# Four step sums in flight and a gather ring of 14 chunks in a four-layer graph network

## What is computed

```
h = relu(layernorm(x))
# layer 0: two graph convolutions (self-loops, 1/sqrt(deg) on both sides)
h = segment_sum((h @ W)[src] * dinv[src] * dinv[dst], dst) + b     # twice
# layer 1: 8 capsules of 16 features, three rounds of routing
z = xc[src];  u = xc
for _ in range(3):
    p = softmax(einsum('ecd,ecd->ec', z, u[dst]));  u = l2norm(segment_sum(z * p, dst) + xc)
# layer 2: mean of the neighbours
h = relu(where(deg > 0, segment_sum(h[src], dst) / deg, h) @ W + b)
# layer 3: messages with three edge attributes
m = gelu(concat(h[src], attr) @ W1 + b1) @ W2 + b2
h = layernorm(h + segment_sum(m, dst)) * gamma + beta
```

## Time and profile before

| | us |
|---|---|
| runs (3) | 6747.69, 6748.66, 6758.79; median 6748.66 |
| profiled execution, from the first to the last instruction | 7795.8 |
| busy in it: PE / DVE / ACT / POOL | 4038 / 3242 / 1099 / 4491 |

### The profile page before, as it was taken

How to read it: one execution, slowest core, us unless ns; L and a number is a source line. 1 busy time by engine, 2 the same in 40 slices (tenths; PEclk the granted TensorE clock), 3 DMA queues, 4 the chain that set the end, 5 groups by cost and what they waited for, 6 DMA issues and landing times.

```text
span 7795.8 us, 105357 instructions
## 1 busy us (share of the span) xinstructions
PE 4038.3 (52%) x24944; PEld 3239.4 (42%) x24945; DVE 3241.9 (42%) x8240; ACT 1099.4 (14%) x2520; POOL 4491.4 (58%) x4619
## 2 busy tenths in 40 slices
PE   0333334333333455555558868823333347777776
PEld 0323323333233345544557767713333334444443
DVE  4222213222124555555578888842221243333335
ACT  0000000000001222222233343310000021111112
POOL 4666665666664555555535535546666635555553
PEclk9656656556566676667789989955665565555555
DMA  3111112111111333333347757711111111111111
GB/s 98 44 45 45 45 46 54 44 46 45 45 45 29 118 118 119 118 118 119 120 151 224 225 176 228 223 47 44 45 45 45 45 41 38 38 39 38 39 38 39
DMA packets 354854, 637.41 MB, mean 82 GB/s; under 512 B 85485, under 2 KB 120442, under 8 KB 354170
## 3 DMA queue, kind: packets, MB, share of 16 engines
q0 software_dynamic: 127936, 263.97, 13.5%
q10 hardware_dynamic: 105408, 191.94, 7.9%
q1 hardware_dynamic: 121466, 181.04, 6.8%
HBM read 500.81 MB, written 135.79 MB: 82 GB/s over the span
## 4 chain that ended last, share of the span: by engine, by line
another core or an unknown queue 35%; PE 24%; issue 16%; DVE 12%; DVEq 5%; DMA 4%; ACT 3%; ACTq 1%; SPq 0%; POOL 0%; POOLq 0%
PE ps_sum L606 15%; PE ps_u L661 4%; PE ps_u L639 4%; DMA hots<-hot_rows 3%; DVE zu L1190 2%; DVE onehot L1000 2%; DVEq L241 2%; DVE acc L1014 1%; DVEq L1014 1%; DVE logit L1199 1%; ACT hots L808 1%; PE ps_a L656 1%; DVE prob_n L1174 1%; ACT onehot L818 1%
## 5 line engine op out<-in xcount | busy, mean ns | idle before, releaser
L525 POOL DMA_INDIRECT ring<-table,rows_idx x3920 | 3874.4, 988 | 2436.8 <-issue 1126.9
L606 PE MATMUL ps_sum<-ring,onehot 128*128 x5856 | 1202.3, 380 | 2328.5 <-DVE onehot L1000 1047.7
L606 PEld LDWEIGHTS ps_sum<-ring,onehot 128*128 128x128 f32 x5856 | 1078.6, 280 | 2452.1 <-issue 2450.5
L1014 DVE TENSOR_TENSOR acc<-ps_sum,acc 128x128 f32 x1708 | 492.2, 288 | 3140.0 <-remote 2336.3
L606 PE MATMUL ps_sum<-msg,onehot 128*128 128x128 f32 x7808 | 1479.8, 349 | 33.3 <-POOL msg L311 21.9
L606 PEld LDWEIGHTS ps_sum<-msg,onehot 128*128 128x128 f32 x7808 | 1285.1, 249 | 432.0 <-issue 396.5
L639 PE MATMUL ps_u<-u_parts,hots 128*128 x8784 | 763.8, 239 | 790.1 <-ACT hots L808 364.8
L1000 DVE SCALAR_TENSOR_TENSOR onehot<-dst,minus_row,iota 128x512 f32<-128x512 f32 x1220 | 913.8, 749 | 239.8 <-issue 211.9
L639 PEld LDWEIGHTS ps_u<-u_parts,hots 128*128 128x128 bf16 x8784 | 619.9, 106 | 915.0 <-issue 880.4
L311 POOL TENSOR_TENSOR msg<-ring,prob_n 128x512 f32<-128x512 f32 x488 | 516.9, 1059 | 614.6 <-DVE prob_n L1174 581.8
L1190 DVE TENSOR_TENSOR zu<-ps_u,ring 128x512 f32<-128x512 f32 x732 | 503.1, 687 | 594.8 <-remote 283.8
(11 more groups left out here) (149 smaller groups left out, 1919.9 us busy)
## 6 DMA issues: line engine op xcount, KB each, us to landing
hots<-hot_rows ACTq DMA_DIRECT2D x488, 256.0 KB, 3.5
ring<-z_rows SPq DMA_DIRECT2D x392, 256.0 KB, 3.6
ring<-table,rows_idx POOLq DMA_INDIRECT x3920
hot_rows<-hots ACTq DMA_DIRECT2D x244, 256.0 KB
z_rows<-ring SPq DMA_DIRECT2D x196, 256.0 KB
table<-acc SPq DMA_DIRECT2D x9, 1024.0 KB, 5.1
x<-in_x SPq DMA_DIRECT2D x1, 3328.0 KB, 11.6
table<-h SPq DMA_DIRECT2D x4, 832.0 KB, 4.4
```

Of the source, the lines that this page charges most:

```text
L525: nc.gpsimd.indirect_dma_start(out=ring[:, j, t * P:(t + 1) * P], out_offset=None, in_=tables[p], in_offset=bass.IndirectOffsetOnAxis(ap=r ...
L606: last = nc.tensor.matmul(ps_sum[k % 2][:, 0:P], lhsT=onehot[:, k % HOTS, t, :], rhs=rows(t), start=(t == 0), stop=(t == TILES - 1))
L1014: V.tensor_tensor(acc_flat[:, at], ps_sum[k % 2][:, 0:P], acc_flat[:, at], ALU.add)\
```

## The change

- In CONV1, CONV2, MEAN and EDGE the ring has 14 slots (`FAR`), and it lies in `u_parts` (`far_flat`) instead of `ring`. CAPS1 keeps the 7 slots of `ring`.
- In these passes SP returns chunk j - 7 behind the publication of chunk j (`far_round`), and POOL waits for the slot of the chunk 14 before.
- The plain passes (not EDGE) sum in four PSUM tiles, `plain_sums`; PE waits for the add of the step four before, and DVE adds three steps behind the onehot.
- `tmp` can't be used ahead of EDGE any more, so deg * BO is added by 52 operations, one per block.
- `rows_idx` holds 14 chunks; `key_row` and `chunk_tab` become 16 bits wide.

```diff
+FAR = 2 * RING
+SLOTS = {CONV1: FAR, CONV2: FAR, CAPS1: RING, CAPS2: RING, CAPS3: RING, MEAN: FAR, EDGE: FAR}
+        far_flat = u_parts[:, :, :, :].rearrange("p b k f -> p (b k f)").bitcast(fp32)[:, 0:FAR * TILES * P]
-        rows_idx = sb("rows_idx", [P, 2, RING, TILES], i32)
+        rows_idx = sb("rows_idx", [P, 2, FAR, TILES], i32)
-        key_row = sb("key_row", [1, CHUNKS], i32)
+        key_row = sb("key_row", [1, CHUNKS], u16)
-        chunk_tab = sb("chunk_tab", [1, 256], i32)
+        chunk_tab = sb("chunk_tab", [1, 256], u16)
+        plain_sums = (ps_sum[0], ps_sum[1], ps_u[0], ps_u[1])
...
+                def far_round(q, first):
+
+                    c0 = q * FAR
+                    for half in range(2):
+                        frees = not first or half
+                        if frees:
+                            keys = keys_of(c0 + (half - 1) * RING, RING)
+                        for j in range(RING):
+                            publish(half * RING + j, q)
+                            if frees:
+                                free(keys[j], None, None)
...
-                    for j in range(RING):
+                    for j in range(slots):
                         if not first:
-                            pool.wait_ge(slot_free, r * RING + (before_this + j + 1 - RING))
+                            pool.wait_ge(slot_free, r * slots + (before_this + j + 1 - slots))
...
-            def sum_step(s, k, p, rows):
+            def sum_step(s, k, p, rows, sums=ps_sum):
                 pe.wait_ge(hot_ready, s + (1 + STEPS * p))
-                if not (s.fixed and s + STEPS * p < 2):
-                    pe.wait_ge(step_added, s + (STEPS * p - 1))
+                if not (s.fixed and s + STEPS * p < len(sums)):
+                    pe.wait_ge(step_added, s + (STEPS * p + 1 - len(sums)))
...
             def plain_pass(p):
+                ahead = len(plain_sums) - 1
+
                 def body(s, k, chunk, have):
                     if have(0):
                         hot(s, k, chunk(0), p)
-                    if have(1):
-                        add_step(s.back(1), k - 1, chunk(1), p)
-                over_steps(dve, ENGINE.DVE, body, 1)
+                    if have(ahead):
+                        add_step(s.back(ahead), k - ahead, chunk(ahead), p, plain_sums)
+                over_steps(dve, ENGINE.DVE, body, ahead)
...
-            link(V.tensor_tensor(tmp, per_feature(BO, NB), per_row(deg[:, :], [P, NB, P]), ALU.mult))
-            link(V.tensor_tensor(h[:, :, :], h[:, :, :], tmp, ALU.add))
+            for b in range(NB):
+                last = V.scalar_tensor_tensor(out=h[:, b, :], in0=BO[:, :], scalar=deg[:, b:b + 1],
+                                              in1=h[:, b, :], op0=ALU.mult, op1=ALU.add)
+            link(last)
```

More of the change, by code:

```diff
@@ L42, with uses_before @@
 GATHERS = (CONV1, CONV2, CAPS1, MEAN, EDGE)
+SLOTS = {CONV1: FAR, CONV2: FAR, CAPS1: RING, CAPS2: RING, CAPS3: RING, MEAN: FAR, EDGE: FAR}
+def uses_before(p, j, kind):
+    return sum(CHUNKS // SLOTS[g] for g in kind if g < p and j < SLOTS[g])
 def build(nc, x_in, src_in, dst_in, dst_rows_in, row_last_in, last_row_in, last_col_in, attr_in, w1, b1, w2, b2, w_mean, b_mean,
           w_edge, b_edge, w_out, b_out, gamma, beta, out):
-    fp32, bf16, i32 = mybir.dt.float32, mybir.dt.bfloat16, mybir.dt.int32
+    fp32, bf16, i32, u16 = mybir.dt.float32, mybir.dt.bfloat16, mybir.dt.int32, mybir.dt.uint16
     ALU = mybir.AluOpType
@@ L182, in build @@
         free_seen = sem("free_seen")
-        rows_in = [sem(f"rows_in{j}") for j in range(RING)]
+        rows_in = [sem(f"rows_in{j}") for j in range(FAR)]
         rows_loaded = [sem(f"rows_loaded{j}") for j in range(RING)]
@@ L246, in block_of, with ring_at, ring_of, slot @@
             return ((s + 0) - chunk).with_bounds(min_val=0, max_val=BLOCKS - 1)
-        def ring_at(chunk):
-            return (chunk % RING) * (TILES * P)
+        def ring_at(chunk, p=CAPS1):
+            return (chunk % SLOTS[p]) * (TILES * P)
+        def ring_of(p):
+            return far_flat if SLOTS[p] == FAR else ring_flat
+        def slot(p, j):
+            return ring_of(p)[:, j * TILES * P:(j + 1) * TILES * P]
         class Step:
@@ L453, in _ @@
                     for j in range(RING - LAG, RING):
-                        publish(j, ROUNDS - 1)
-                for j in range(0 if loads else RING - LAG, RING):
-                    free(keys[j], j, ROUNDS - 1)
+                        publish(j, rounds - 1)
+                for j in range(0 if loads or SLOTS[p] == FAR else RING - LAG, RING):
+                    free(keys[j], j, rounds - 1)
             for g0, g1 in CUTS:
@@ L512, in _, with round_of @@
                 before_this = CHUNKS * p
-                def round_of(r, half, first, last, n=n, p=p, before_this=before_this):
-                    pool.wait_ge(idx_staged, r + (1 + ROUNDS * n))
+                slots, rounds = SLOTS[p], CHUNKS // SLOTS[p]
+                staged_before = sum(CHUNKS // SLOTS[g] for g in GATHERS[:n])
+                def round_of(r, half, first, last, p=p, before_this=before_this, slots=slots,
+                             staged_before=staged_before):
+                    pool.wait_ge(idx_staged, r + (1 + staged_before))
                     pool.sem_inc(idx_seen, 1)
-                    for j in range(RING):
+                    for j in range(slots):
                         if not first:
-                            pool.wait_ge(slot_free, r * RING + (before_this + j + 1 - RING))
+                            pool.wait_ge(slot_free, r * slots + (before_this + j + 1 - slots))
                             pool.sem_inc(free_seen, 1)
-                        if j == RING - 1 and not last:
-                            stage(r + 1, 1 - half)
+                        if j == slots - 1 and not last:
+                            stage(r + 1, 1 - half, slots)
                         for t in range(TILES):
                             nc.gpsimd.indirect_dma_start(
-                                out=ring[:, j, t * P:(t + 1) * P], out_offset=None, in_=tables[p],
+                                out=slot(p, j)[:, t * P:(t + 1) * P], out_offset=None, in_=tables[p],
                                 in_offset=bass.IndirectOffsetOnAxis(ap=rows_idx[:, half, j, t:t + 1],
@@ L1285, in edge_body @@
                     V.tensor_tensor(zu[:, one, :], ps_u[one][:, :],
-                                    ring_flat[:, ds(ring_at(chunk(1)), TILES * P)], ALU.add)\
+                                    ring_of(EDGE)[:, ds(ring_at(chunk(1), EDGE), TILES * P)], ALU.add)\
                      .then_inc(pre_ready, 1)
```

41 lines of the change are left out of this document (21 added, 20 removed).

## The result

| | us |
|---|---|
| kernel before, 4 runs | 6749.4 (6747.7 to 6758.8) |
| changed kernel, 4 runs | 6940.7 (6935.3 to 6946.7) |
| ratio, 95% interval | 1.0283 (1.0269 to 1.0298) |
| profiled run of the changed kernel: time, span | 6941.8, 6939.6 |

The change costs 191 us. The forecast was 6743, and its range ended at 6795.

The account below looks back on a forecast made before the run. The prediction took GpSimd's gathers, 1.25 us apart, to bound the gather passes in the runs, TensorE in EDGE. From 6748.7 us, index copies (-3) and EDGE's lead-in (-3), all else 0, gave 6743 us, range 6560 to 6795.

Parts of the forecast that it names:

- Narrower tables (u16) and more semaphores: Term for the 16-bit tables and added semaphores: they change only loads of registers, 0 us.
- Rival B: GpSimd's longer loop body is refetched, 20 stalls of 2.2 us in four passes: 44 us slower, 6793 us; chance 0.11.
- hardly any slot waits: Step: GpSimd's waits for ring slots, 1023 us in the profile, are mostly absent from the timed runs.
- the prediction's 980: GpSimd's floor for a gather pass: 784 gathers starting 1.25 us apart, 980 us.
- The prediction's mark: Profile after: plain-pass slot waits from 131 us to under 30, span about 300 us or more lower, runs hardly moving.
- Rival A: Part of the slot waits is real in the runs, so removing them in plain passes gives 6574 us; chance 0.30.
- Rival C: Late sums come in such bunches that four buffers don't help; runs stay at 6749 us; chance 0.06.
- Four sums, 0: Term for four sums in flight in the plain passes: GpSimd's 4.0 us a step covers the loop, 0 us.
- ring, 0: Term for the 14-slot ring: 0 where slots are never short, up to 349 us for plain passes otherwise.
- EDGE's loop, 0: EDGE pass: TensorE, busy 1047 of 1380 us at half clock, bounds it, so a longer ring gives 0 us.
- Index copies, -3: Fourteen fewer index copies in each of four passes, 0.07 us each: -3 us, ends 0 and -4.
- EDGE's lead-in, -3: Ahead of EDGE, 52 operations of 128 columns take 11.1 us instead of 14.2: -3 us, ends -7 and +1.

Follow-up runs that it names:

- e15: Kernel before with only the chunk table narrowed to 16 bits, on a chip with prompt sums: 6947.0 us, 1.0286 of the kernel before.
- e13: Kernel before plus a mask (255) on the values waited against, on a chip with prompt sums: 6747.2 us, 0.9987 of the kernel before.
- e2: Changed kernel with both tables at 32 bits and masked waits, on a chip with late sums: 7886.3 us, 1.0042 of the kernel before.
- e5: Changed kernel with 32-bit tables and masked waits, on a second chip with late sums: 7887.7 us, 1.0033 of the kernel before.
- e9: Changed kernel with 32-bit tables and masked waits, on a third chip with late sums: 7896.6 us, 1.0042 of the kernel before.
- e1: Kernel before plus a mask (255) on the values waited against, on a chip with late sums: 7875.3 us, 1.0026 of the kernel before.
- e4: Kernel before with 32-bit tables and masked waits, on a second chip with late sums: 7873.1 us, 1.0023 of the kernel before.
- e14: Changed kernel with 32-bit tables and masked waits, on a chip with prompt sums: 6752.1 us, 0.9996 of the kernel before.
- e12: Changed kernel with ring of 7 in all passes, chunk table 32-bit with mask, key table 16-bit, prompt sums: 6763.1 us, 1.0015 of the kernel before.

## Why the prediction was wrong

**The step that failed** is the last edit: "Narrower tables (u16) and more semaphores change only loads of registers: 0." They do change loads of registers only, but those loads are on the path, and the term is not 0: the 16-bit chunk table alone costs 193 us (e15), the whole change 191. No duration of a load was read, and no rival had one, so the range had nothing on this side beyond B's 44 us. Two things in the profile of before spoke against the zero. Its load rows gave 1.1 us for a load of 16 values. And in the chain that ended last, which the prediction doesn't use, the load is an item of its own:

```profile
PE ps_sum L606 15%; PE ps_u L661 4%; PE ps_u L639 4%; DMA hots<-hot_rows 3%; DVE zu L1190 2%; DVE onehot L1000 2%; DVEq L241 2%; DVE acc L1014 1%; DVEq L1014 1%; DVE logit L1199 1%; ACT hots L808 1%; PE ps_a L656 1%; DVE prob_n L1174 1%; ACT onehot L818 1%
```

"DVEq L241 2%" is 1.7% before rounding, about 133 us of the 7796. (On a chip with prompt sums, in e13, it is 41 us.) The factor of three could not have been known, but a bound could: 40 rounds in CAPS2 and CAPS3 with nothing of DVE's beside the load, so each microsecond more on a load is at least 40 us. The prediction also named only the passes that the diff rewrites. The tables are read in all seven, and nearly all of the loss lies in two that its sum has no term for.

**Slots and late sums.** The prediction takes it "that the runs have hardly any slot waits and that their gather passes stand at GpSimd's pace". For the plain passes this was right. In e13 the plain passes have no slot wait and take 991, 997 and 999 us from first to last gather, by the prediction's 980 and some stretched gathers. In EDGE 103 us of slot waits remain. The reason given was wrong. It is not the profiled execution that differs from the runs: in every set the profiled run's time was within 0.3% of its kernel's median. What differs is the chip, or a state that lasted as long as it was used. The prediction's mark, slot waits of a plain pass down from 131 us to under 30 and a span lower by about 300 or more, seemed fulfilled and better (none left, 856 us less), but not because of the change: that was luck. Where sums are late, ring and four sums leave the slot waits of a plain pass at 105 to 120 us (e2, e5, e9), from 129 to 137 (e1, e4).

**Rival A** (part of the slot waits is real in the runs) is refuted for prompt sums. Where they are real, the change doesn't remove them, so its 6574 had no chip to come true on. The gathers' 1.25 us held on all chips; the estimate from the Trainium skill's figure of about 1 us would have been 200 us a pass too low.

**Rival B** (GpSimd refetching a longer body) did not happen. GpSimd's "issue" gaps in the first plain pass of the changed kernel are 0.3 us at the longest, and in EDGE 0.7. The sign was right by another mechanism: loads of registers on the streams of DVE, TensorE and GpSimd.

**Rival C** (late sums come in bunches that four buffers don't help) comes close to what happens where sums are late: +15 and +11 us for the whole of the change at 32 bits (e5 against e4, e2 against e1). Four buffers do help a little there, by 37 us alone, and the ring takes it back. The timed chips had no late sums for it to act on.

**Four sums, 0; ring, 0; EDGE's loop, 0**: right where sums are prompt, +5 us in all with the two gains below (e14 against e13). In EDGE the long ring lets GpSimd finish 42 us earlier (first to last gather 1132.4 in e13, 1090.2 in e14), but from the first add to the last there are only 4.5 us less (1142.8 and 1138.3). The likely reason is that TensorE is what runs through. e13's window of the gathers:

```profile
5520.95:6653.38 1132.43, 1021.69 (x2615) 544.29 (x2616) 450.08 (x959) 189.99 (x480) 788.41 (x811) 0.50 0.17 45
```

TensorE is busy 1022 of 1132 us at half the clock, where the earlier trace rows had 1047 of 1380: on a chip with prompt sums the bound that the prediction named is plainer still.

**Index copies, -3**: not found. The three plain passes in e14 take 996, 999 and 997 us. The stretching of gathers varies by more from pass to pass than 4 us.

**EDGE's lead-in, -3**: the 52 operations take this long (duration of one in ns, and the whole in the timeline, where the earlier trace rows had 2 x 7.09):

```profile
L1302 DVE SCALAR_TENSOR_TENSOR h<-BO,deg,h x52: 346/351/355, 5714.4 to 5727.8; 128x128 f32<-128x128 f32 x52
```

```profile
5714.41 13.75 DVE L1302 SCALAR_TENSOR_TENSOR h<-BO,deg,h 128x128 f32<-128x128 f32 x52
```

13.75 us against 14.2 is -0.4, inside the ends -7 and +1 and close to the upper one. One operation costs 0.264 us from start to start, so the middle of the two bounds (0.21) was no good choice: the row nearest in kind, the 128-column add at 0.29, was closer.

## What to carry to other kernels

A load of registers is an instruction on the engine's own stream. Price it from its row, and count the rounds in which the engine has nothing beside it. Narrowing the two tables here saved under a kilobyte and tripled each load of the chunk table, so measure such a load before narrowing a table that it reads, and count its rounds where the engines' chain is tight. When a profile is 15% longer than the runs it belongs to, look for what differs before reading prices out of it: here the waits that the change was aimed at were missing from the plain passes of the timed runs. And where the consumer of a ring sets the pace, a longer ring only moves work that the consumer must still do after the last gather.

## What the runs showed of the hardware

- A load of 4, 8 or 16 values on DVE takes 0.35, 0.60 and 1.1 us from a 32-bit table and 0.95, 1.83 and 3.6 us from a 16-bit one: about 0.06 and 0.22 us a value. TensorE (0.34, 0.59, 1.1 and 0.99, 1.92, 3.8) and GpSimd (16 values: 1.06 and 3.58) do the same. The Trainium skill ("DMA: Bandwidth & Descriptors", "Latency and other measured facts") has a floor of about 600 ns for such a load. The rows go below it, to 0.34 us, and the floor says nothing of the width.
- SyncE's loads of the key table, read on chips with prompt sums, show that the width is not all. (On the others their durations scatter.) Each begins 7 keys further on than the last. From the 32-bit table every fourth, the one that begins at a multiple of 28 keys (112 bytes), takes 0.93 us for 7 keys (e14) and 1.17 for 14 (e13), the three between 1.47 and 2.87. From the 16-bit table all take 1.45 (changed kernel) and 2.86 (e12), those at multiples of 28 keys too. The chunk table is always read from a multiple of 4 values, 16 bytes at 32 bits. So the short kind of load seems to want 32-bit values and a start at a multiple of 16 bytes in the table, on any engine. No run moved a table to test this, and why it is so stays open.
- Five chips fall into two kinds. On three, a plain pass's semaphore of a sum arrives on average 3 to 4 us and up to 19 us after the last recorded matmul before it (kernel before and e1, e4; about 205 of the 244 updates of a pass are recorded there); on two, 0.01 us after it. It shows in all passes that gather, less in CAPS1 (1.6 us) and EDGE (0.8), and not in CAPS2 and CAPS3 (0.01 us on both kinds). The kernel before takes 1100 us (16%) more on the three, nearly all of it in the passes that gather (e1 against e13: 150 to 157 us in each plain pass, 396 in CAPS1, 209 in EDGE). That the late semaphores are the cause is argued from this and not shown by a run. What delays them was not found and not tried.
- Masking the values waited against, `v & 255`, costs 20 to 26 us where sums are late and nothing that can be told where they are prompt (-7 us, within 0.2%).
